# A Mamba-2 decoder layer on one NeuronCore: a pipeline of groups of eight tiles becomes a pipeline of single tiles, with decays from spread rows

## The reference

```
n    = layernorm(x);  h = n * rsqrt(mean(n^2) + eps) * norm_w      # [512 tokens, 512]
proj = h @ in_proj_w.T                                             # 8192 gate, 8192 hid, 1024 B, 1024 C, 128 dt
hid, B, C = silu(causal_conv4(...))                                # four taps and a bias per channel
dt   = softplus(dt + dt_bias);  A = -exp(A_log)
A_cs = cumsum(A * dt)                                              # per head, along the sequence
M    = (C_i . B_j) * exp(A_cs_i - A_cs_j)  for j <= i, else 0      # scores times decays, per head
y    = M @ (hid * dt) + D * hid
out  = rmsnorm_per_group(y * silu(gate)) * gnorm_w @ out_proj_w.T  # 8 groups of 1024 channels, 16 heads each
x    = x + layernorm(x) + out
x    = x + fake_quant(layernorm(x)) @ fake_quant(context)          # context [2, 512, 512]
x    = x + unpermute(gelu(permute(layernorm(x)) @ up) @ down)      # 16 heads of 32 features
```

## Time and profile before

| | |
|---|---|
| median of 3 runs | 919.98 us (919.88 to 920.33) |
| span of the profiled execution | 918.4 us |
| mean granted TensorE clock | 0.970 of full speed |
| PE busy | 860.0 us (94%) |
| DVE busy | 682.9 us (74%) |
| ACT busy | 540.8 us (59%) |
| POOL busy | 469.7 us (51%) |
| DMA | 61.56 MB, 67 GB/s |

### The profile page before, as it was taken

How to read it: one execution, slowest core, us unless ns; L and a number is a source line. 1 busy time by engine, 2 the same in 40 slices (tenths; PEclk the granted TensorE clock), 3 DMA queues, 4 the chain that set the end, 5 groups by cost and what they waited for, 6 DMA issues and landing times.

```text
span 918.4 us, 15226 instructions
## 1 busy us (share of the span) xinstructions
PE 860.0 (94%) x4666; PEld 649.8 (71%) x4666; DVE 682.9 (74%) x939; ACT 540.8 (59%) x1004; POOL 469.7 (51%) x366
## 2 busy tenths in 40 slices
PE   4888899999999999999999999999999999888478
PEld 3676577777778777877777777877787777656255
DVE  7796799559982989379965998299937996597753
ACT  3533688348853777357834885377735783566343
POOL 6335267536665458345753566535834575555020
PEclk9999799999999999999999999999999999889779
DMA  5223012211223122221222121212222222401001
GB/s 145 76 76 92 24 48 94 81 59 56 84 63 91 50 65 74 79 63 51 93 68 71 47 90 61 90 46 70 73 80 58 56 92 64 146 24 35 0 1 46
DMA packets 34656, 61.56 MB, mean 67 GB/s; under 512 B 4740, under 2 KB 5252, under 8 KB 34628
## 3 DMA queue, kind: packets, MB, share of 16 engines
q1 hardware_dynamic: 34628, 61.21, 22.1%
HBM read 59.75 MB, written 1.44 MB: 67 GB/s over the span
## 4 chain that ended last, share of the span: by engine, by line
issue 40%; PE 26%; POOL 21%; DVE 7%; ACT 3%; POOLq 1%; DMA 1%; SPq 0%; DVEq 0%; ACTq 0%
POOL w_lo L464 12%; POOL sqsum L486 5%; PE ps_in L1141 4%; PE ps_in L1143 4%; PE ps_in L1142 4%; PE ps_o L1141 3%; PE ps_o L1143 2%; PE ps_o L1142 2%; POOL wo_lo L470 2%; POOL eB L479 2%; PE ps_t L1200 1%; PE ps_t L1207 1%; PE ps_y L1270 1%; PE ps_df L1239 1%; PE ps_in L1423 1%
## 5 line engine op out<-in xcount | busy, mean ns | idle before, releaser
L1141 PE MATMUL ps_in<-h_hi,w_hi 128*128 128x512 f32 x544 | 226.1, 416 | 5.3 <-DVE hid L869 2.1
L464 POOL TENSOR_TENSOR w_lo<-raw,w_hi 128x512 fp32r<-128x512 f32 x144 | 187.2, 1322 | 71.9 <-ACT w_hi L563 71.6
L1142 PE MATMUL ps_in<-h_lo,w_hi 128*128 128x512 f32 x544 | 214.3, 394 | 0.0
L1143 PE MATMUL ps_in<-h_hi,w_lo 128*128 128x512 f32 x544 | 214.1, 394 | 0.0
L479 POOL TENSOR_TENSOR eB<-eB,gmB 128x512 f32<-128x512 f32 x64 | 98.1, 1532 | 207.0 <-ACT eB L610 207.0
L869 DVE SCALAR_TENSOR_TENSOR hid<-ps_in,curc,hid 128x510 f32<-128x510 f32 x180 | 134.4, 746 | 18.1 <-ACT hid L583 13.1
L602 ACT ACTIVATE ps_df<-ps_df 128x256 f32<-128x256 f32 x185 | 74.2, 430 | 119.2 <-PE ps_df L1239 118.3
L1141 PEld LDWEIGHTS ps_in<-h_hi,w_hi 128*128 128x128 f32 x544 | 102.8, 189 | 42.0 <-issue 17.9
L470 POOL TENSOR_TENSOR wo_lo<-rawo,wo_hi 128x512 fp32r<-128x512 f32 x64 | 83.4, 1309 | 75.8 <-ACT wo_hi L568 75.1
L1143 PEld LDWEIGHTS ps_in<-h_hi,w_lo 128*128 128x128 f32 x544 | 103.0, 189 | 22.8
L1142 PEld LDWEIGHTS ps_in<-h_lo,w_hi 128*128 128x128 f32 x544 | 103.2, 190 | 17.9
(11 more groups left out here) (257 smaller groups left out, 1524.4 us busy)
## 6 DMA issues: line engine op xcount, KB each, us to landing
raw<-in_w_in SPq DMA_DIRECT2D x144, 256.0 KB, 2.8
rawo<-in_w_out SPq DMA_DIRECT2D x64, 256.0 KB, 2.7
res<-in_x SPq DMA_DIRECT2D x4, 256.0 KB, 3.6
out_x<-res SPq DMA_DIRECT2D x4, 256.0 KB, 2.2
raw<-in_ctx SPq DMA_DIRECT2D x3, 256.0 KB, 3.4
mov<-acs_parts SPq DMA_DIRECT2D x32, 12.0 KB
sta<-acs_parts SPq DMA_DIRECT2D x32, 12.0 KB
th<-in_ctx SPq DMA_DIRECT2D x2, 256.0 KB, 4.2
```

The costliest lines, as they stand in the source:

```text
L464: pool.tensor_tensor(w_lo[:, i % W_RING, :], raw[:, i % RAW_RING, :], w_hi[:, i % W_RING, :].bitcast(F32), ALU.subtract).then_inc(s_lo, 1)
L1141: pe.matmul(dst, lh, rh, start=first, stop=False)
L1142: pe.matmul(dst, lh, rl, start=False, stop=False)
L1143: return pe.matmul(dst, ll, rh, start=False, stop=last)
```

## The change

The unit of the pipeline is one tile instead of one group. There are 64 steps; in step t (of group n) PE does outputs of the tile two back, the hid projection of this one, the turn of the one before, the output projection of the one three back, and the gate projection. The next group's B tile is projected in step 3, its C tile in step 5. `hid`, `gate`, `z_hi` and `z_lo` become rings of four tiles, `hdt` of two; `ps_in` has two banks for projections and `ps_o` four for the output sums alone.

The decay differences are no longer matmuls. The cumulative sums are stored once to DRAM in fp32, and for each tile SP spreads its two heads' rows over all 128 partitions into `e` (ring of four; 1536 values a partition, 768 KB). POOL masks the two diagonal blocks with `affine_select`, in which masked places get -1e30, and ACT takes exp with the row's own negative sum (`nag`) as a bias: eight instructions a tile. The clamp (Relu) goes away, and the scores need no mask.

The context is loaded and quantised in the eight steps of group 0, by POOL (three passes a block), into a tensor of its own. The one-hot tiles are made by POOL behind the last group. In the prologue the dt projection comes ahead of B and C. The sum of q2 for the quantised product stands in the last steps of the drain.

```diff
-W_RING, RAW_RING = 6, 3
+W_RING, RAW_RING = 6, 6
 WO_RING, RAWO_RING = 4, 2
+E_RING = 4
+MASKED = -1e30
...
+def lagged(n, t, lag):
...
+            def load_rows(m, q):
+
+                u = CT * m + q
+                wait(sp, s_y, u - E_RING + 1)
+                row = acs_dram[bass.ds(2 * u, 2), :, :, :].rearrange("h k b i -> (h k b i)")
+                sp.dma_start(e[:, q % E_RING, :, :, :, :].rearrange("p h k b i -> p (h k b i)"),
+                             row.partition_broadcast(P)).then_inc(s_rows[q % E_RING], 16)
...
+            def mask_rows(m, q):
+
+                for k in (0, 2):
+                    d = e[:, q % E_RING, :, k, :, :]
+                    last = pool.affine_select(out=d, in_=d, compare_op=ALU.is_ge, fill=MASKED, base=0,
+                                              pattern=[[0, 2], [0, BATCH], [1, P]], channel_multiplier=-1)
+                last.then_inc(s_msk, 1)
...
+                if not (is_first(n) and t < 2):
+                    decays_off(*lagged(n, t, 1))
+                    rows_arrived(n, t)
+                    split_out(m, q)
+                    mask_rows(n, t)
+                if len(tiles) > 2:
+                    split_in(ahead[0], tiles[2])
...
+            def exps(m, q):
+
+                u = CT * m + q
+                act.wait_ge(s_msk, u + 1)
+                if q == 0:
+                    act.wait_ge(s_curg, 2 * m + 2)
+                for late in (0, 1):
+                    for hh in range(2):
+                        for b in range(BATCH):
+                            h = 2 * q + hh
+                            a = e[:, q % E_RING, hh, 2, b, :] if late else e[:, q % E_RING, hh, 0:2, b, :]
+                            last = act.activation(a, a, ACT.Exp, bias=nag[:, 2 * b + late, h:h + 1])
+                    last.then_inc(s_exp, 1)
...
+            def decays_diagonal(m, q):
+
+                u = CT * m + q
+                dve.wait_ge(s_exp, 2 * u + 2)
+                if q == 0:
+                    dve.wait_ge(s_gm, 2 * m + 2)
+                a = e[:, q % E_RING, :, 0::2, :, :].rearrange("p h k b i -> p h k (b i)")
+                g = gm[:, 0::2, :, :].rearrange("p k b i -> p k (b i)").unsqueeze(1)\
+                    .broadcast_to([P, 2, 2, BATCH * P])
+                dve.tensor_tensor(a, a, g, ALU.mult).then_inc(s_ma, 1)
...
+            def step(n, t):
+                tiles = step_tiles(n, t)
+                lead = is_first(n) and t < 3
+                if t == 2 and not is_first(n):
+                    token_sums(n - 1)
+                if not lead:
+                    outputs(*lagged(n, t, 2))
+                project(n, tiles[0])
...
+                if not lead:
+                    turn(*lagged(n, t, 1))
+                    out_tile(*lagged(n, t, 3))
+                if t == 0 and not lead:
+                    scores(n)
+                for tile in tiles[1:]:
+                    project(n, tile)
```

More of the change, by code:

```diff
@@ L422, in _ @@
+            for t in range(CT):
+                step(GROUPS - 1, t)
+            load_out(GROUPS - 1, CT - 1)
+            sp.wait_ge(s_olo, STEPS)
             sp.dma_start(up_raw, up).then_inc(s_ffw, 16)
@@ new lines, in start_residual, with step @@
+            def start_residual(k):
+                pool.wait_ge(s_u, k + 1)
+                pool.tensor_tensor(res[:, k, :], res[:, k, :], u_in[:, k, :], ALU.add).then_inc(s_res, 1)
+            def step(n, t):
+                if t == 2 and not is_first(n):
+                    group_rms(n - 1)
+                ahead = (n, t + 1) if t + 1 < CT else (n + 1, 0)
+                tiles = [] if is_last(n) and t + 1 == CT else step_tiles(*ahead)
+                lead = is_first(n) and t < 3
+                if tiles:
+                    split_in(ahead[0], tiles[0])
+                m, q = lagged(n, t, 2)
+                if q and not lead:
+                    add_square(m, q)
+                if tiles:
+                    split_in(ahead[0], tiles[1])
+                if is_first(n) and t == 2:
+                    rows_arrived(0, 0)
+                    mask_rows(0, 0)
+                    rows_arrived(0, 1)
+                    mask_rows(0, 1)
+                    decays_off(0, 0)
+                if not (is_first(n) and t < 2):
[5 more added lines that the diff above has]
+                    split_in(ahead[0], tiles[2])
+                if is_first(n):
+                    if t == 0:
+                        for k in range(TT):
+                            start_residual(k)
+                    context(t)
@@ new lines, in _ @@
+            for j in range(2):
+                split(j, j)
+            for tile in step_tiles(0, 0):
+                split_in(0, tile)
+            for t in range(CT):
+                step(0, t)
+            with pool.Fori(1, GROUPS - 1) as n:
+                for t in range(CT):
+                    step(n, t)
+            for t in range(CT):
+                step(GROUPS - 1, t)
+            last_m = GROUPS - 1
+            add_square(last_m, CT - 2)
+            split_out(last_m, CT - 2)
@@ new lines, in _ @@
+            decays_off(last_m, CT - 1)
+            split_out(last_m, CT - 1)
+            add_square(last_m, CT - 1)
+            pool.wait_ge(s_iota, 2)
+            pool.wait_ge(s_pk, 2)
+            pool.wait_ge(s_in, LEAD + NIN * GROUPS - 2)
+            for k in range(DK):
+                pool.tensor_scalar(take[:, k, :], perm_row[:, :], dcol[:, k:k + 1], None, ALU.is_equal)\
+                    .then_inc(s_tp, 1)
+                pool.tensor_scalar(put[:, k, :], iota_row[:, :], perm_col[:, k:k + 1], None, ALU.is_equal)\
+                    .then_inc(s_tp, 1)
@@ new lines, in _ @@
+            for c in range(2):
+                tanh_of(c, c, bc[:, c, :])
+            for t in range(CT):
+                step(0, t)
+            with act.Fori(1, GROUPS - 1) as n:
+                for t in range(CT):
+                    step(n, t)
+            for t in range(CT):
+                step(GROUPS - 1, t)
+            last_m = GROUPS - 1
+            gate_tanh(last_m, CT - 1)
+            z_high_and_square(last_m, CT - 2)
+            exps(last_m, CT - 1)
+            cast_out(last_m, CT - 2)
@@ L1374, in _ @@
+            project_tile(0, 0, ps_in[:, 0, :])
+            project_tile(1, 1, ps_in[:, 1, :])
+            for t in range(CT):
+                step(0, t)
+            with pe.Fori(1, GROUPS - 1) as n:
+                for t in range(CT):
+                    step(n, t)
+            for t in range(CT):
+                step(GROUPS - 1, t)
+            last_m = GROUPS - 1
+            outputs(last_m, CT - 2)
+            turn(last_m, CT - 1)
+            out_tile(last_m, CT - 3)
             pe.wait_ge(s_q2, BATCH * DK)
-            pe.wait_ge(s_exp, 3 * CT * GROUPS)
+            pe.wait_ge(s_taps, LEAD + NCONV * GROUPS - 2)
```

1286 lines of the change are left out of this document (574 added, 712 removed).

## The result

The changed kernel takes 987.59 us in the median of 4 runs (985.94 to 994.73) against 920.15 us before: a ratio of 1.0749 with a 95% interval of 1.0712 to 1.0786. It is slower, by 67 us. Its profiled span is 986.2 us.

What follows compares the result with a forecast made beforehand. A circle of outputs, projection, exps, silu and decay product was to bind most steps: 63.5 + 65.3 + 6 x 96.5 + 90.5 + 15.6 + 4 + 69.8 = 887.7 us, plus 10 for lock waits; 899 measured, range 865 to 938.

Steps and rivals of the forecast that it cites:

- PE's own work: PE's instruction stream in the group loop: 90 us a group without difference matmuls, against 99.65 before.
- circle of a regular step: Loop from outputs through PE, ACT and DVE back to outputs: 10.65 us without collision, 11.05 with one wait.
- Exps: ACT's eight exps a tile, within the circle: 2.8 us, bounds 1.8 and 5.7.
- masks: POOL's two masks a tile: 0.9 us each, bounds 0.29 and 1.29.
- projection of h(t), result at about 4.6: Opening of the circle on PE: outputs to 1.45 us, then the h projection, done about 4.6 us into the step.
- the lock: DVE and POOL passes go through one at a time: 0.4 us a regular step, plus 0.22 in 46 steps.
- rival 1: DVE loses the lock to POOL at the decay product in every regular step: 12.0 us, 936 measured; chance 0.26.
- Partly in its idle time: 11.85: Steps behind B and C: DVE's three more taps and silu, 2.8 us partly in idle time, make 11.85 us.
- Step 0: First step of a group, with params and masked scores on DVE ahead of the next outputs: 12.35 us.
- the 1.3 us: Addition in step 0 for params and masked scores on DVE, copies of dtg and nag included.
- One-hots: Eight POOL passes ahead of group_rms at the end: 0.75 us each, about 4 us late (1 to 8).
- The start: First outputs at 61 us, step 3 at 63.5 (58 to 75); group 0's steps 3 to 7 65.3, context about 4.

Runs made afterwards that it cites:

- e12: On top of e10, DVE does turned ahead of the taps of h instead of behind them: 893.08 us, ratio 0.9694.
- e6: Changed kernel with DVE's turned and decay product of the tile before ahead of both silus instead of behind them: 959.11 us, ratio 1.0432.
- e5: Changed kernel with DVE's gated ahead of skip_and_gate and POOL's splits and square adding on 16 columns, computation partly left out: 911.86 us, ratio 0.9923.
- e7: Changed kernel with gated ahead of skip_and_gate, turned and decay product ahead of the silus, and one-hots on DVE: 909.61 us, ratio 0.9894.
- e2: Changed kernel with POOL's weight splits (from group 1 on) and square adding on 16 columns, computation partly left out: 950.53 us, ratio 1.0325.
- e10: On top of e7, DVE masks the scores in step 0 before copying the group's dt and decay columns: 906.28 us, ratio 0.9861.
- e3: Changed kernel with the eight one-hot passes moved from POOL to DVE, ahead of the last skip_and_gate: 978.55 us, ratio 1.0656.
- e13: On top of e12, two of the context's three POOL passes cover 16 of 512 columns, most quantisation left out: 882.5 us, ratio 0.959.
- e4: Changed kernel with the context loaded and quantised by POOL in the last group instead of group 0: 1000.85 us, ratio 1.0868.

## Why the prediction was wrong

The direction and the range were both missed: 899 us forecast, 865 to 938 at the outside, 987.6 measured. Step by step:

1. **PE's own work was right.** A group of it was put at 90 us; e12 shows 90.55. Taking the difference matmuls off PE frees what was said.
2. **The circle of a regular step was right within 0.3 us**, 10.65 to 11.05 us: 10.82 in step 2, where e6 takes it down to PE's 10.3 in two groups by moving the decay product out of the circle, and 10.8 to 10.9 in step 7 without the low clock. Step 1 (11.1) is PE's own work in every run. Exps were put at 2.8 us, and eight take 2.87; masks at 0.9, they take 0.63 undisturbed.
3. **The step that failed is "projection of h(t), result at about 4.6".** It took the bank as free. In steps 4 and 6 it is that of the last gate tile, and the projection starts 2.2 us late, behind two DVE passes that wait for the outputs themselves. The prediction listed which tiles fall into which step, but didn't follow the banks. This wait and the lock of 4, with the clock behind them, make 62.5 of the loop's 63.9 us (e5).
4. **The lock was put in the wrong steps.** I priced it at 0.4 us in each regular step and as a rival with the decay product lost everywhere. In regular steps the race for the decay product was won, but by 0.10 us in steps 0 to 3 (697.05 against 697.15) and by 0.01 in steps 5 and 7 (685.24 against 685.25): that rival 1 did not come true in every step is luck. The lock was lost in steps 4 and 6, where three more taps and a silu make DVE late: 3.2 and 3.6 us a step. "Partly in its idle time: 11.85" holds only if DVE isn't held up. e5 takes 3 and most of 4 away and gives 96.3 us a group for 96.5 on file, 580.4 for 579. That it meets the sum so closely is in part luck: steps 1 and 2 together are 1.0 under the forecast, steps 0 and 6 0.6 and 0.3 over it. And e7 shows that the lock need not be taken away: with gated and the decay product first on DVE the loop takes 578.0 us beside a full POOL. So the circle was not unavoidable in steps 4 and 6; the order on DVE made it longer there.
5. **PE's clock was left out.** 12 of 48 steps at about 1.4 us each, some 17 us of the 64. All twelve are steps 4 to 7, in or behind the waits of 3 and 4. The clock column of the earlier trace rows is lower where PE waits for others, and I didn't carry that over to a loop with waits.
6. **Step 0**: 12.35 forecast, 14.6 measured. The copies blocked behind the split (1.28 for 0.21 in e2) and the scores' wait for `turned`, 1.7 us, since they share a PSUM bank, were both unseen: the copies were counted in the 1.3 us, but at their undisturbed price. e10 gave 0.4 us, e12 another 1.6.
7. **One-hots**: the mechanism was right, the size not. 0.75 us each had no row of such a pass behind it; they take 1.54 from one start to the next, 12.3 us instead of about 6 ahead of `group_rms`. e3 gives 11.5 us back, more than the 10.6 by which the end was over.
8. **The start**: 20.5 us more. For the context's passes, 4.6 us of POOL a step, the sum has 4 us over all five steps. e13 shows 8.2 us in steps 3 to 7 for 60% of them, on top of e12; in the changed kernel itself e4 took all of them away and won 5.7. The outputs of tile 0 began at 68.4 instead of 61. The rows were in time: the sums were ready at 41.0 us (40 forecast), the third spread had landed at 53.5 (53 forecast). But POOL's masks began only at 61.7, in its fixed order behind splits and the context's second block, and ACT's exps at 63.5. Without the context (e4) the masks begin at 58.2, but the exps at 62.4, behind ACT's tanh of tile 2, and the outputs at 69.8: the place in the order of each engine sets the start, not POOL alone. What part of this the lock has in the prologue, where four residual sums on POOL (1.6 us each) run beside DVE's chain to dt and the silus of B and C, wasn't tried apart.

Rival 1 named the right side and one of the mechanisms, the lock, but in the wrong steps; the bank wait and the clock aren't in it, and its 936 us would have been too low as well. That the spreads of rows cost time was no part of it: a spread lands 4.4 us after its issue in the median, and no wait for one stands in the trace. Where the expected gain went: PE's 8.4 us a group were freed, but a group with 90 us of PE work now takes 107.2 (642.9 over six), held up by bank, lock and clock, against 99.65 before; late one-hots and the start of group 0 add to it at both ends.
